# Both heads' attention scores in two row tiles of TensorE, with a reordered step, on Trainium2

## What is computed

```
xn = layernorm(x)
q, k, v = xn @ Wq, xn @ Wk, xn @ Wv              # 16 heads of 64
q, k = rotary(q), rotary(k)
s = softmax(causal(q @ k.T) / 8) @ v ; s = s @ Wo
g = silu(((xn * (r @ in_scale)) @ sign(W).T) * (r @ out_scale) + bias), r = softmax(xn @ gate_w.T)
out = x + s * g
```

## Time and profile before

| | |
|---|---|
| median of 3 runs | 1186.87 us (1186.68 to 1187.99) |
| the profiled execution, its own time | 1189.66 us |
| its span, first to last instruction | 1187.4 us |
| busy: PE / weight loads (PEld) / DVE / ACT / POOL | 96% / 80% / 61% / 52% / 36% |
| mean granted clock of TensorE | 0.984 of full |

### The profile page before, as it was taken

One profiled execution on the slowest core, in us unless ns is written; L12 is line 12 of the kernel. 1 busy time (PEld: TensorE's weight loads), 2 busy tenths in 40 slices (PEclk: granted clock), 3 DMA queues, 4 the chain that ended last, 5 costly groups with the idle time before them and its releaser, 6 DMA issues.

```text
span 1187.4 us, 17857 instructions
## 1 busy us (share of the span) xinstructions
PE 1142.3 (96%) x5736; PEld 954.0 (80%) x5736; DVE 729.4 (61%) x1735; ACT 616.2 (52%) x1291; POOL 432.1 (36%) x258
## 2 busy tenths in 40 slices
PE   4699999999999999999999999999999998999998
PEld 3477777788888888888888888888888886888886
DVE  7676553357776777767767777767767777323133
ACT  5445344155666556656566466655665666322111
POOL 2526427433433424235333343342523523332220
PEclk9799999999999999999999999999999998999999
DMA  6734232302202022021460220202202025555652
GB/s 205 283 107 189 77 107 76 120 0 73 62 9 62 9 71 62 9 62 36 176 212 9 69 59 13 62 9 71 62 9 62 26 72 186 164 182 179 209 196 104
DMA packets 86983, 111.23 MB, mean 94 GB/s; under 512 B 3304, under 2 KB 68840, under 8 KB 85936
## 3 DMA queue, kind: packets, MB, share of 16 engines
q1 hardware_dynamic: 86960, 110.93, 28.7%
HBM read 77.37 MB, written 33.55 MB: 93 GB/s over the span
## 4 chain that ended last, share of the span: by engine, by line
PE 87%; DVE 6%; ACT 3%; POOL 2%; issue 1%; DMA 1%; SPq 0%; DVEq 0%; ACTq 0%; POOLq 0%
PE at_proj L44 17%; PE at_proj L46 17%; PE at_proj L45 17%; PE at_out L909 7%; PE at_pt L896 6%; PE ff_z_ps L264 6%; PE at_score L878 3%; PE at_score L879 3%; PE at_score L44 2%; PE at_score L45 2%; PE at_score L46 2%; PE at_proj L863 1%; POOL ff_xs_lo L601 1%; DMA w_stage<-in_L_ffn_weight_dram 1%; ACT xn_hi L365 1%
## 5 line engine op out<-in xcount | busy, mean ns | idle before, releaser
L44 PE MATMUL at_proj<-xn_hi,w_hi 128*128 128x512 f32 x896 | 363.4, 406 | 2.9 <-ACT at_v_t L1014 2.9
L46 PE MATMUL at_proj<-xn_hi,w_lo 128*128 128x512 f32 x896 | 352.0, 393 | 0.0
L45 PE MATMUL at_proj<-xn_lo,w_hi 128*128 128x512 f32 x896 | 350.8, 392 | 0.0
L46 PEld LDWEIGHTS at_proj<-xn_hi,w_lo 128*128 128x128 f32 x896 | 169.0, 189 | 37.6
L44 PEld LDWEIGHTS at_proj<-xn_hi,w_hi 128*128 128x128 f32 x896 | 169.5, 189 | 33.3 <-issue 3.3
L45 PEld LDWEIGHTS at_proj<-xn_lo,w_hi 128*128 128x128 f32 x896 | 169.8, 190 | 30.4
L1273 POOL TENSOR_TENSOR at_turning<-at_turning,rope_table 128x512 f32<-128x512 f32 x64 | 82.9, 1296 | 305.1 <-DVE at_turning L1144 305.1
L1281 POOL TENSOR_TENSOR w_lo<-w_stage,w_hi 128x1024 fp32r<-128x1024 f32 x45 | 114.5, 2559 | 162.8 <-ACT w_hi L993 162.8
L1031 ACT ACTIVATE at_prob<-at_score,at_neg_max 128x512 f32<-128x512 f32 (+3 forms) x256 | 133.4, 526 | 68.0 <-DVE at_neg_max L1172 67.6
L1040 ACT ACTIVATE at_pt_hi<-at_pt 128x512 fp32r<-128x512 f32 (+1 forms) x192 | 94.0, 524 | 101.1 <-PE at_pt L896 100.4
L1189 DVE TENSOR_TENSOR at_pt_lo<-at_pt,at_pt_hi 128x512 fp32r<-128x512 f32 (+1 forms) x192 | 111.8, 597 | 43.7 <-ACT at_pt_hi L1040 42.8
(11 more groups left out here) (129 smaller groups left out, 1827.7 us busy)
## 6 DMA issues: line engine op xcount, KB each, us to landing
z_store<-z SPq DMA_DIRECT2D x16, 512.0 KB, 2.7
w_stage<-in_L_attn_Wq_dram SPq DMA_DIRECT2D x16, 512.0 KB, 3.8
w_stage<-in_L_attn_Wk_dram SPq DMA_DIRECT2D x16, 512.0 KB, 5.1
w_stage<-in_L_attn_Wv_dram SPq DMA_DIRECT2D x16, 512.0 KB, 6.1
att_store<-at_att_t SPq DMA_DIRECT2D x32, 256.0 KB, 2.0
rope_table<-att_store SPq DMA_DIRECT2D x16, 512.0 KB, 6.5
z<-_attn_hidden_states_dram SPq DMA_DIRECT2D x16, 512.0 KB, 4.5
at_turning<-z_store SPq DMA_DIRECT2D x16, 512.0 KB, 6.1
```

The costliest lines, as they stand in the source:

```text
L44: pe.matmul(out, sh, mh, start=first, stop=False)
L45: pe.matmul(out, sh, ml, start=False, stop=False)
L46: return pe.matmul(out, sl, mh, start=False, stop=final)
```

## The change

Scores are done for both heads at once, in three units (`SCORE_UNITS`: widths 512; 384 and 128; 256). q's and k's parts are plain full tiles, [128, 512] high and low, and each head's rows are a 64-row operand: three products (high*high, low*high, high*low) for each head, issued alternately for rows 0 to 63 and 64 to 127, into different PSUM banks. That makes 24 matmuls per step with 64 rows in place of 16 with 128. `k_hh`, `k_l0` and the zeroing go. ACT rounds q and k with one full-height activation each, and DVE subtracts with one each. The three units stand at three places of PE's step. Both heads are normalised one after the other, ahead of the reading of k's projection; POOL splits the first weight ahead of q's rotation (b = 1), and in the last step both rotations stand ahead of the Wo splits. The end after the loop is reordered alike. Of PE's, ACT's, DVE's and POOL's lists the new lines are shown; the old ones are in the code above.

```diff
-SCORE_BANKS = (((3, 0),), ((2, 0), (0, 384)), ((1, 0),))
-
-PT_BANKS = (((0, 0),), ((1, 0), (3, 384)), ((2, 0),))
+SCORE_UNITS = (((3, 0),), ((2, 0), (0, 384)), ((1, 0),))
+PT_UNITS = (((0, 0),), ((1, 0), (3, 384)), ((2, 0),))
 PT_WIDTH = (512, 512, 256)
...
+def score_bank(u, h):
+    return (2 * u + h) % 3
...
+def pt_bank(h, u):
+    return (3 * h + u) % 2
...
-        qk = sb("at_qk", [P, 2, 6, SEQ], F32R)
-        q_st, k_hh, k_l0 = ([[qk[:, p, c + h, :] for h in range(2)] for p in range(2)] for c in (0, 2, 4))
+        qk = sb("at_qk", [P, 2, 2, 2, SEQ], F32R)
+        qk_hi, qk_lo = ([[qk[:, p, c, part, :] for c in range(2)] for p in range(2)] for part in (PHI, PLO))
...
-        zeroed = sem("at_zeroed")
...
+            def scores(a, u, parity):
+                if u == 0:
+                    pe.wait_ge(qk_ready, 2 * a + 2)
+                (q_hi, k_hi), (q_lo, k_lo) = qk_hi[parity], qk_lo[parity]
+                for h in range(2):
+                    if later(score_entry(a, u, h), 3):
+                        pe.wait_ge(expd, score_entry(a, u, h) - 2)
+                for t, col in SCORE_UNITS[u]:
+                    width = (t + 1) * P
+                    for n, (q, k) in enumerate(((q_hi, k_hi), (q_lo, k_hi), (q_hi, k_lo))):
+                        for h, rows in enumerate(pair_rows):
+                            last = pe.matmul(score_ps[score_bank(u, h)][:, col:col + width], q[rows, t * P:(t + 1) * P],
+                                             k[rows, 0:width], start=(n == 0), stop=(n == 2))
+                            if n == 2 and (t, col) == SCORE_UNITS[u][-1]:
+                                last.then_inc(scored, 1)
+
...
                 project(i, s, b, 0, range(0, KT // 2))
                 if later(s, 1):
                     v_transposes(s - 1)
+                    scores(s - 1, 0, 1 - b)
                 if later(s, 2):
-                    prob_transposes(2 * s - 3, 1, (2,))
+                    prob_transposes(s - 2, 1, (2,))
                 project(i, s, b, 0, range(KT // 2, KT))
+                if later(s, 1):
+                    scores(s - 1, 1, 1 - b)
                 if later(s, 2):
-                    values(s - 2, 2 * s - 3, 1, b)
-                if later(s, 1):
-                    scores(s - 1, 0, 1 - b)
-                project(i, s, b, 1)
-                if later(s, 1):
-                    scores(s - 1, 1, 1 - b)
-                    prob_transposes(2 * s - 2, 0, (0, 1))
-                project(i, s, b, 2, range(0, KT - 3))
-                if later(s, 1):
-                    prob_transposes(2 * s - 2, 0, (2,))
-                project(i, s, b, 2, range(KT - 3, KT))
-                if later(s, 1):
-                    values(s - 1, 2 * s - 2, 0, 1 - b)
-                    prob_transposes(2 * s - 1, 1, (0, 1))
+                    values(s - 2, 1, b)
+                project(i, s, b, 1, range(0, 3))
+                if later(s, 1):
+                    scores(s - 1, 2, 1 - b)
+                project(i, s, b, 1, range(3, KT))
+                project(i, s, b, 2, range(0, 3))
+                if later(s, 1):
+                    prob_transposes(s - 1, 0, (0, 1))
+                project(i, s, b, 2, range(3, 6))
+                if later(s, 1):
+                    prob_transposes(s - 1, 0, (2,))
+                project(i, s, b, 2, range(6, KT))
+                if later(s, 1):
+                    prob_transposes(s - 1, 1, (0, 1))
+                    values(s - 1, 0, 1 - b)
 
...
+            scores(s - 1, 0, 1)
+            prob_transposes(s - 2, 1, (2,))
+            output(0, 0, 0, range(0, 4), first=True)
+            values(s - 2, 1, 0)
+            scores(s - 1, 1, 1)
+            scores(s - 1, 2, 1)
+            output(0, 0, 0, range(4, 6), first=True)
+            output(0, 0, 1, range(4, 6))
+            prob_transposes(s - 1, 0, (0, 1))
+            output(0, 0, 0, range(6, 7), first=True)
+            prob_transposes(s - 1, 0, (2,))
+            prob_transposes(s - 1, 1, (0,))
+            output(0, 0, 1, range(6, 7))
+            prob_transposes(s - 1, 1, (1,))
+            values(s - 1, 0, 1)
+            prob_transposes(s - 1, 1, (2,))
+            values(s - 1, 1, 1)
...
-            def q_high(s, b):
-                act.wait_ge(rot_done, 2 * s + 1)
-                if later(s, 2):
-                    act.wait_ge(scored, 6 * (s - 1))
-                for h, rows in enumerate(pair_rows):
-                    last = act.activation(q_st[b][h][rows, :], rotated[0][rows, :], ACT.Copy)
-                last.then_inc(high_done, 1)
-
-            def k_high(s, b, h):
-                act.wait_ge(rot_done, 2 * s + 2)
-                for dup in pair_rows:
-                    last = act.activation(k_hh[b][h][dup, :], rotated[1][pair_rows[h], :], ACT.Copy)
-                if h == 1:
-                    last.then_inc(high_done, 1)
+            def high(s, b, c):
+                act.wait_ge(rot_done, 2 * s + c + 1)
+                if c == 0 and later(s, 2):
+                    act.wait_ge(scored, score_entry(s - 1, 0, 0))
+                act.activation(qk_hi[b][c], rotated[c][:], ACT.Copy).then_inc(high_done, 1)
...
             def step(i, s, b, spare):
+                if later(s, 2):
+                    pt_hi_parts(s - 2, 1, (1,))
+                    copy_low_half(s - 2, 0)
                 if later(s, 1):
                     v_hi(s - 1, 1 - b)
                 if later(s, 2):
+                    pt_hi_parts(s - 2, 1, (2,))
+                if later(s, 1):
+                    exps(s - 1, 0)
                 if b == 1:
                     spare(i, 0)
+                if later(s, 2):
+                    copy_low_half(s - 2, 1)
+                if later(s, 1):
+                    exps(s - 1, 1)
+                    exps(s - 1, 2)
+                high(s, b, 0)
+                if later(s, 1):
+                    pt_hi_parts(s - 1, 0, (0, 1))
+                if spare is output_weights and b == 1:
+                    att_hi(0, 0)
                 if b == 1:
                     spare(i, 1)
+                if later(s, 1):
+                    pt_hi_parts(s - 1, 0, (2,))
+                high(s, b, 1)
+                v_copy(s)
+                if later(s, 1):
+                    pt_hi_parts(s - 1, 1, (0,))
+                if b == 1:
                     spare(i, 2)
...
-            def q_low(s, b):
-                dve.wait_ge(high_done, 2 * s + 1)
-                for h, rows in enumerate(pair_rows):
-                    last = dve.tensor_tensor(q_st[b][h][pair_rows[1 - h], :], rotated[0][rows, :], raw(q_st[b][h][rows, :]),
-                                             ALU.subtract)
-                last.then_inc(qk_ready, 1)
-
-            def k_low(s, b):
-                dve.wait_ge(high_done, 2 * s + 2)
-                for h, rows in enumerate(pair_rows):
-                    last = dve.tensor_tensor(k_l0[b][h][rows, :], rotated[1][rows, :], raw(k_hh[b][h][rows, :]), ALU.subtract)
-                last.then_inc(qk_ready, 1)
+            def low(s, b, c):
+                dve.wait_ge(high_done, 2 * s + c + 1)
+                dve.tensor_tensor(qk_lo[b][c], rotated[c][:], raw(qk_hi[b][c]), ALU.subtract).then_inc(qk_ready, 1)
...
+            def maxima(a, u):
+                for h in range(2):
+                    dve.wait_ge(scored, score_entry(a, u, h) + 1)
...
             def step(i, s, b):
+                if later(s, 2):
+                    pt_low_parts(s - 2, 1, (1,))
+                    merge(s - 2, 0, b)
+                if later(s, 1):
+                    maxima(s - 1, 0)
                     v_low(s - 1, 1 - b)
                 if later(s, 2):
+                    pt_low_parts(s - 2, 1, (2,))
                 rotate_read(s, 0)
+                if later(s, 1):
+                    maxima(s - 1, 1)
                 if later(s, 2):
+                    merge(s - 2, 1, b)
+                if later(s, 1):
+                    maxima(s - 1, 2)
+                    normalise(s - 1, 0)
+                    normalise(s - 1, 1)
                 rotate_read(s, 1)
+                low(s, b, 0)
+                if later(s, 1):
+                    pt_low_parts(s - 1, 0, (0, 1, 2))
+                low(s, b, 1)
+                if later(s, 1):
+                    pt_low_parts(s - 1, 1, (0,))
 
             dve.wait_ge(keep["z_add"], BATCH * QT)
-                dve.memset(raw(k_l0[p][0][HEAD_DIM:P, :]), 0.0).then_inc(zeroed, 1)
-                dve.memset(raw(k_l0[p][1][0:HEAD_DIM, :]), 0.0).then_inc(zeroed, 1)
...
+            s = STEPS
+            pt_low_parts(s - 2, 1, (1,))
+            merge(s - 2, 0, 0)
             wo_lo(2)
+            maxima(s - 1, 0)
             v_low(s - 1, 1)
+            pt_low_parts(s - 2, 1, (2,))
             wo_lo(3)
+            maxima(s - 1, 1)
+            merge(s - 2, 1, 0)
             wo_lo(5)
+            maxima(s - 1, 2)
+            normalise(s - 1, 0)
+            normalise(s - 1, 1)
```

(12 more changed lines are left out.)

177 lines of the change are left out of this document (53 added, 124 removed).

## The result

The changed kernel takes 1205.39 us (median of 4 runs, 1204.15 to 1206.62); the kernel before, run beside it on the same chip, 1186.78 (4 runs, 1183.62 to 1187.99). The ratio is 1.0159, 95% interval 1.0138 to 1.018: +18.6 us where +7.2 was forecast. The sign is right, the time lies in the range and in the likeliest case's own range, and the size is wrong by more than two to one.

What follows compares the result with a forecast made beforehand. The prediction took PE's own work to bound the loop. Loop +14.0, start -4.8 and end -2 gave +7.2 on 1189.66, so 1196.9; the runs' median being 2.8 lower, it forecast 1194.1 us, range 1162 to 1224.

Steps and rivals of the forecast that it cites:

- the likeliest case: Whole kernel: heads run side by side, each height change costs 0.36 us; 1194 us, own range 1186 to 1212; chance 0.40.
- the scores' stream: Scores in the loop: 1.89 us a step instead of 2.52, if both heads' matmuls and loads overlap; 0.63 saved.
- C: Rival for the scores: matmuls overlap but weight loads do not, 2.64 us a step; 1217.3 us; chance 0.19.
- D: Rival for the scores: row height changes but nothing overlaps, 3.78 us of scores a step; 1252.6 us; chance 0.08.
- the changes of height: Score units in the loop: 128 to 64 rows and back three times a step, 0.36 us each, 1.08 together.
- B: Rival for the loop: going from 128 to 64 rows does not empty the array; 1160.6 us; chance 0.28.
- the loop's sum: Loop: a step gains 0.63 and loses 1.08, so +0.45 us; over 31 steps +14.0 us.
- ACT and DVE at nothing: Loop: work saved by fewer copies on ACT and DVE is off the path and costed at nothing.
- E: Rival for the loop: ACT or DVE overruns the 0.4 us slack, PE waits each step; 1203 us; chance 0.05.
- the start: Start of the loop: k read earlier shortens PE's wait by 2.0 us and avoids half clock, 2.8 more; -4.8 us.
- the end: Last step and after: old normalising wait goes, some 2 us of new wait comes; -2 us, between -6 and +3.
- The named wait: After the loop: PE waits some 2 us for POOL's attention split before the first output matmul.

Runs made afterwards that it cites:

- full-height kernel: Changed kernel's order on every engine, but with the old full-height score operands and 16 matmuls of 128 rows: 1201.66 us, ratio 1.0126 to the kernel before.
- act_order_last: Changed kernel with ACT's rounding of Wo blocks in the last step moved behind the probability parts: 1202.58 us, ratio 1.0131 to the kernel before.
- the fourth switch: Changed kernel with score unit 1 cut in two by a projection block, one more height change a step: 1218.86 us, ratio 1.028 to the kernel before.
- wo_split_first: Changed kernel with POOL's first Wo split put ahead of both rotations in the last step only: 1199.14 us, ratio 1.0100 to the kernel before.

## Why the prediction was right and wrong

**Right: what bounds the kernel.** The loop is PE's own work before and after; the intervals between matmuls in a step show no wait.

**Right: the scores' stream.** The choice of 1.89 us rested on two heads running side by side, which no row of before showed. Pairs 0.23 us apart and loads of six in 0.53 show it. This refutes rivals C and D: the loads of units 0 and 1 take 0.53 + 0.93 us and those of unit 2 0.41, 1.87 in all and not 2.64. The reading of Part 3 of the page "TensorE: Matmul & The Clock Gate" (the Trainium skill), which the prediction had weighed beside its sum, falls too. By its rule a load overlaps only matmuls of other row groups, which by the estimate gave 1226 (the working of its 2.9 us a step is not shown); measured was 1205. That row groups overlap, the trace agrees; that their own rows bar it, neither rows 5 nor the six loads in 0.53 us bear out.

**Right: the changes of height.** 0.36 each was taken; the sum from the rows is 1.08 for three, the forecast's own figure, and a fourth costs 0.43, inside the bounds of 0.27 to 0.55. That it came out to the hundredth is luck: 0.36 was picked between bounds a factor of two apart, from a change to 16 rows. B, with free switches, is refuted. The loop alone turns at 0.63/3 = 0.21 a switch, and the forecast's loop, start and end together at 0.28; the measured 0.36 is above both.

**Nearly right: the loop's sum.** Forecast +0.45 a step, measured +0.501 in the mean and +0.51 in the middle of the loop. The forecast took head 1's scores (1.26 us) for both heads, but head 0's, behind `values`, take 1.32 (607.07 to 608.39), so the tiling saves 2.58 - 1.89 = 0.69 and not 0.63. Against that, projection matmuls now stand behind `values` twice a step, and the second of them comes after 0.28 and 0.29 instead of 0.23: 0.11. Rows give -0.69 + 1.08 + 0.11 = +0.50; the remaining 0.01 is below what rows of 0.01 us can share out. So the forecast left out two terms, -0.06 and +0.11, which partly cancel. Over 30 steps its +13.5 became +15.0.

**Right, with an unnamed cover: ACT and DVE at nothing, E not seen.** No wait of unit 2 on ACT shows. But the full-height kernel shows that in the new order DVE's slack is so thin that its old subtractions cost 0.25 us a step. The prediction named the idle third of both engines as the cover; in the new order it is the shorter subtractions that keep DVE's low parts in time.

**Right: the start.** -4.8 forecast, -4.5 measured, idle 0.78 for 0.8 forecast, no half clock.

**Wrong: the end.** This is the failed step: "-2 us, between -6 and +3". The ledger's end is +6.6, and the last of the prediction's 31 loop sets (0.5) lies in it, so its term came out at +6.1. The walk put POOL's works behind each other (rotations, Wo's two splits, the attention split) and asked who waits for the attention split. The old wait did go as forecast: both normalisings take 1.28 us each there (987.08 and 988.48). But the walk didn't ask what the moved split itself lets go: SP's next Wo load waits for the staging slot, ACT's queue for that load, and the probability parts stand in ACT's queue behind it. The sentence that excused it, "SP's lists do not change; their weight loads wait on POOL's splits ... used a step on", is true in the loop, where a slot is filled a step ahead, and false in the last step, where Wo's blocks are used as they come. The named wait was real (2.02 in act_order_last) and was hidden by the one that wasn't named. "The hand-woven remainder looks 2 us shorter" had the right sign at most: with the split moved back the end is 0.2 under that of before, with 1.0 of two longer steps' scores in it, so the rest is 1.2 shorter, with 6.4 us of idle time on PE where before had 5.9; the prediction counted only 2.10 of these.

The sum again with the measured terms: loop 15.5 for 14.0, start -4.5 for -4.8, end +6.1 for -2, on the profiled execution's 1189.66: 1206.8, where the profiled execution of the kernel after took 1206.57.

**Still open.** The 0.43 for the fourth switch against 0.36 on average for the three: the cut unit has 128-column parts, whose weight loads may show more, and no run took these alone. Why a change of height costs PE anything, beyond the 0.35 us in which the load engine stands, no run shows. The end's bounds were too narrow as well: they came from the waits found, which say nothing of a chain that was not walked.

## What to carry to other kernels

When an instruction is moved, follow what it releases as well as what it needs: the slot it frees, the transfer that fills that slot, the engine whose queue holds the reader of the transfer, and everything queued behind that reader. Do it separately for the steady loop and for the last step, where nothing is used "a step later". By these numbers, tiling rows to use a half-empty array pays only if the row-tiled work stands in few, long stretches: here three short stretches a step cost 1.08 us to save 0.69. And a wait removed by moving work off one slot can reappear where the work lands (2.10 became 2.81; an idle slot's subtraction became 2.17 on PE): look at what is beside the new place first.

## What the runs showed of the hardware

- Matmuls of two row groups (64 rows each, outputs in different banks) run side by side at full rate, a pair per 0.23 us at 512 columns, and their loads too, six in 0.53 us. It doesn't depend on the order of issue: three products of one head ahead of three of the other take 0.97 us, against 0.96 in turns.
- A change between 128 and 64 rows costs about 0.36 us for the way in and out together, in one run 0.43; ahead of the first load behind the change the load engine idles 0.35 to 0.36 us, the same as for 16 rows (0.17 where transposes stand ahead, at unit 0).
- DVE can be slowed beside POOL where all of its operands are in SBUF: a pair of subtractions of 1.39 us took 2.39 to 3.95, and normalising of 1.28 us took 2.03 or 4.15 beside POOL's splits. It matters which of the two starts first. In the kernel before 16 subtractions start 0.07 us ahead of a split on POOL, which then takes 2.88 us in place of 2.40 (the row at 976.93), while each of them keeps its 0.69. In the kernel after the one at 600.15 starts 1.29 us into a split and takes 1.67 us. The low parts of the probabilities (`pt_low_parts`), which read PSUM, kept theirs in every case (0.68 to 0.70 us at 512 columns, in the kernels before and after, with POOL at work or not).
- The clock after a wait of PE: after 0.78 and 1.57 us it stayed full. After 2.02 us (act_order_last) the next five matmuls lasted 0.50, 0.39, 0.40, 0.50 and 0.63 us: three at full clock, and the lower level from the fourth or fifth on. After 2.39 us (wo_split_first) they lasted 0.49, 0.59 and 0.63. After 2.89 us (kernel before) and 5.76 us the lower level held from the start.
